# Twelve more fields looked up by one-hot rows in place of gathers, small buffers in shared homes

## The reference, cut to what matters

```python
e = stack([tbl_f[ids[:, f]] for f in range(39)], axis=1)      # 512 x 39 x 16
x0 = xk = e
for W in (W0, W1):                                            # two layers, 128 outputs each
    xk = einsum('bid,bjd,ijh->bhd', x0, xk, W.reshape(39, -1, 128))
    outs.append(xk)
z = sum(concatenate(outs, axis=1), axis=-1)                   # 512 x 256
h = concatenate([z, dense_ctx], axis=1)
h = maximum(h @ W_top1 + b_top1, 0); h = maximum(h @ W_top2 + b_top2, 0)
y = h @ W_top3
```

## Time and profile before

| what | value |
|---|---|
| median of 3 runs | 377.59 us (377.39 to 378.48) |
| span of the profiled execution | 376.0 us |
| TensorE busy | 227.8 us (61%) |
| VectorE, ScalarE busy | 159.5 us, 156.7 us (42% each) |
| GpSimd busy | 110.4 us (29%), nearly all in 115 gathers of 958 ns |
| first select of the loop on TensorE | 173.95 us |
| granted clock of TensorE | full in all 40 slices |

### The profile page before, as it was taken

One profiled execution on the slowest core, in us unless ns is written; L12 is line 12 of the kernel. 1 busy time (PEld: TensorE's weight loads), 2 busy tenths in 40 slices (PEclk: granted clock), 3 DMA queues, 4 the chain that ended last, 5 costly groups with the idle time before them and its releaser, 6 DMA issues.

```text
span 376.0 us, 4521 instructions
## 1 busy us (share of the span) xinstructions
PE 227.8 (61%) x1601; PEld 173.6 (46%) x1601; DVE 159.5 (42%) x313; ACT 156.7 (42%) x302; POOL 110.4 (29%) x119
## 2 busy tenths in 40 slices
PE   4311101001000010168999899998999999999997
PEld 4200000000000000055667588766778877788897
DVE  4350000000100000037989676897775767756411
ACT  4600000000200000027789766797786677865511
POOL 5777777777777775000000000000000000000000
PEclk9999999999999999999999999999999999999999
DMA  6800000000000000000921000000000000000000
GB/s 177 239 12 9 7 7 6 7 6 7 6 7 6 7 6 6 0 0 3 260 86 40 0 3 2 1 2 0 3 1 2 0 2 2 2 2 0 2 0 2
DMA packets 8218, 8.71 MB, mean 23 GB/s; under 512 B 2951, under 2 KB 5804, under 8 KB 8196
## 3 DMA queue, kind: packets, MB, share of 16 engines
q1 hardware_dynamic: 4516, 7.48, 7.0%
q0 software_dynamic: 3680, 0.95, 2.7%
HBM read 8.42 MB, written 0.00 MB: 22 GB/s over the span
## 4 chain that ended last, share of the span: by engine, by line
PE 50%; issue 36%; ACT 6%; DVE 4%; another core or an unknown queue 2%; DMA 1%; ACTq 0%; DVEq 0%
PE turn_bank L524 10%; PE pair_bank L445 5%; PE x_bank L469 5%; PE g_bank L502 5%; PE x_bank L471 4%; PE x_bank L472 4%; DVE onehot L771 2%; ACT prod_hi L1006 2%; PE g_bank L686 2%; PE x_bank L481 2%; PE turn_bank L562 2%; ACT prod L1001 2%; PE turn_bank L535 1%; PE x_bank L695 1%
## 5 line engine op out<-in xcount | busy, mean ns | idle before, releaser
L420 POOL DMA_INDIRECT emb<-tbl,ids_sb x115 | 110.2, 958 | 37.2 <-issue 34.7
L1001 ACT ACTIVATE prod<-pair_bank 128x512 f32<-128x512 f32 (+1 forms) x112 | 65.8, 599 | 40.8 <-PE pair_bank L445 36.0
L843 DVE TENSOR_TENSOR prod_lo<-prod,prod_hi 128x512 fp32r<-128x512 f32 x96 | 64.8, 685 | 2.7
L469 PE MATMUL x_bank<-prod_hi,pair_w_hi 128*128 128x512 f32 (+1 forms) x112 | 63.1, 564 | 1.8 <-DVE prod_lo L843 1.3
L445 PE MATMUL pair_bank<-x,sel 117*128 117x512 bf16 (+1 forms) x112 | 42.8, 384 | 0.9 <-ACT x L983 0.7
L524 PE MATMUL turn_bank<-g_sb,w_sb 128*128 128x128 f32 x312 | 42.2, 278 | 0.0
L524 PEld LDWEIGHTS turn_bank<-g_sb,w_sb 128*128 128x128 f32 x312 | 39.4, 191 | 3.1 <-issue 1.4
L686 PE MATMUL g_bank<-tab_parts,onehot 125*128 125x96 bf16 x36 | 7.4, 251 | 54.5 <-issue 54.5
L1006 ACT ACTIVATE prod_hi<-prod 128x512 fp32r<-128x512 f32 x64 | 40.1, 626 | 0.1
L471 PE MATMUL x_bank<-prod_lo,pair_w_hi 128*128 128x512 f32 x96 | 37.8, 394 | 0.0
L472 PE MATMUL x_bank<-prod_hi,pair_w_lo 128*128 128x512 f32 x96 | 37.7, 392 | 0.0
(11 more groups left out here) (140 smaller groups left out, 333.4 us busy)
## 6 DMA issues: line engine op xcount, KB each, us to landing
emb<-tbl,ids_sb POOLq DMA_INDIRECT x115
tab<-small SPq DMA_DIRECT2D x2, 560.0 KB
wt<-w_top SPq DMA_DIRECT2D x2, 512.0 KB, 4.5
tab<-small SPq DMA_DIRECT2D x1, 504.0 KB
wa<-pair_w_a SPq DMA_DIRECT2D x1, 448.0 KB
wb<-pair_w_b SPq DMA_DIRECT2D x1, 448.0 KB
wtd<-w_dense SPq DMA_DIRECT2D x1, 256.0 KB
dense_sb<-dense_t SPq DMA_DIRECT2D x1, 256.0 KB
```

The costliest lines, as they stand in the source:

```text
L420: pool.indirect_dma_start(out=emb[:, at:at + D], out_offset=None, in_=tables[f], in_offset=bass.IndirectOffsetOnAxis(ap=ids_sb[:, c * M + ...
L469: mm = pe.matmul(x1_banks[k % 2][:, :], pair_w_hi[p, t, :], hi(n), start=(t == 0), stop=(t == FULL))
L843: dve.tensor_tensor(lo(n), prod[rows, n % RING, :], prod_hi[rows, n % RING2, :], ALU.subtract).then_inc(lo_done, 1)
L1001: act.activation(prod[0:ROWS[t], n % RING, :], pair_bank[n % 2][0:ROWS[t], :], ACT.Square).then_inc(sq_done, 1)
```

## The change

Four more fields of chunk 1 (12 in all) and eight of chunk 3 (where there were none) are looked up; chunks 0 and 2 stay. `PARTS` says how many parts of four fields a chunk has. The gathers of these fields fall away. The loop of chunk 0 gets a third part, read from the second table set, whose parts now stay in memory (`tab_parts1`); the loop of chunk 2 gets two parts. The ids of 28 slots are turned, in groups of eight: two groups in the head as before, two more (eight and four slots) into `turn_bank` at steps n = 8 and n = 10, each copied by ScalarE one step later. The joins of a chunk (`words`) are one call over all its parts, in block j = number of parts at t = 3. z2, h1 and y move into `emb`, h2 into `dense_sb`, the looked-up words of later chunks into `rest`, and the summed pair weights into the early region, where buffers of the loop come later. ScalarE's copy of a looked-up part gets a wait for the split of the chunk before.

```diff
-LOOKED = (3, 1, 1, 0)
+PARTS = (0, 3, 2, 2)
+LATE_AT = (NT + 1, NT + 3)
+SLOTS = LATER * sum(PARTS)
+HEAD_SLOTS = 16
...
         def first_gathered(c):
-            return (0, 8, 16, NS)[LOOKED[c]]
+            return LATER * PARTS[c] if c else NS
...
+            def spread_later(q, bank):
+                for s in range(8 * q, min(8 * q + 8, SLOTS)):
+                    c = [s < LATER * sum(PARTS[:n + 1]) for n in range(NCH)].index(True)
+                    f = s - LATER * sum(PARTS[:c])
+                    mm = pe.transpose(halved(bank)[:, s % 8 * CH:(s % 8 + 1) * CH],
+                                      half_h[:, c, f:f + 1].to_broadcast([128, SP]), eye_h[:, :])
+                mm.then_inc(later_spread, 1)
...
-                if c + 1 < NCH and LOOKED[c + 1]:
-                    if j in (0, 1) and t == NT - 1:
+                if n in LATE_AT:
+                    pe.wait_ge(dense_act, 2)
+                    pe.wait_ge(later_ids_ok, HEAD_SLOTS // 8 + LATE_AT.index(n))
+                    spread_later(HEAD_SLOTS // 8 + LATE_AT.index(n), turn_bank)
+                if c + 1 < NCH:
+                    if j < PARTS[c + 1] and t == NT - 1:
                         wait(pe, x1_done, n // NT)
                         look_up_later(c + 1, j, 0, 2)
-                    if j in (1, 2) and t < 2:
+                    if 1 <= j <= PARTS[c + 1] and t < 2:
                         look_up_later(c + 1, j - 1, 2 * t + 2, min(2 * t + 4, HOT))
...
-                if looks and j < 2 and t >= 2:
+                if j < looks and t >= 2:
                     later_one_hot(c + 1, j, t - 2)
-                if looks and j == 2 and t == 4:
+                if looks and j == looks and t == 3:
                     words(0, c + 1)
...
+            def keep_later_ids(q, bank):
+                act.wait_ge(later_spread, q + 1)
+                s0, s1 = 8 * q, min(8 * q + 8, SLOTS)
+                act.activation(later_ids[:, s0:s1, :].rearrange("p w b -> p (w b)"), halved(bank)[:, 0:(s1 - s0) * CH],
+                               ACT.Copy).then_inc(later_ids_ok, 1)
...
+                if n - 1 in LATE_AT:
+                    keep_later_ids(HEAD_SLOTS // 8 + LATE_AT.index(n - 1), turn_bank)
...
             def keep_looked_later(c, part):
-                act.wait_ge(later_row, HOT * (2 * (c - 1) + part + 1))
+                act.wait_ge(later_row, HOT * (nth(c, part) + 1))
+                act.wait_ge(split_done, pieces(c - 1))
```

More of the change, by code:

```diff
@@ L122, in build_tower @@
         rest = sb("rest", [128, M * D])
+        later_looked = rest[:, 0:LATER * max(PARTS) * E].rearrange("b (f q d) -> b f q d", q=3, d=D)
         parts = sb("parts", [128, D, 3, M], BF16)
@@ L320, in lookups @@
         def lookups(c):
-            return sum(LOOKED[:c + 1])
+            return len(SETS) + sum(parts > 0 for parts in PARTS[:c + 1])
         def gathers(c):
@@ L465, in layer1 @@
                     c, j = divmod(k, NB)
-                    if j in (1, 2) and c + 1 < NCH and LOOKED[c + 1]:
+                    if c + 1 < NCH and 1 <= j <= PARTS[c + 1]:
                         pe.wait_ge(picked, picks(c + 1, j - 1))
@@ L665, in _ @@
                 if f == 7:
[L667 to L671, removed]
+                    for q in range(HEAD_SLOTS // 8):
+                        spread_later(q, later_id_bank[q])
             for n in range(len(SETS)):
@@ L800, in words @@
             def words(n, c=0):
[L802 to L806, removed]
+                f0, w = (0, LATER * PARTS[c]) if c else SETS[n][:2]
+                done = lookups(c) if c else n + 1
+                dve.wait_ge(picked, picks(c, PARTS[c] - 1) if c else n + 1)
+                low, words_in = (later_low[:, 0:w * D], later_looked[:, 0:w, :, :]) if c else (
+                    low_word[:, f0 * D:(f0 + w) * D], looked[:, f0:f0 + w, :, :])
                 dve.scalar_tensor_tensor(low.rearrange("b (f d) -> b f d", d=D), words_in[:, :, 2, :], 256.0,
@@ L885, in step @@
                 splits = j == 3 and c + 1 < NCH
-                looks = c + 1 < NCH and LOOKED[c + 1]
+                looks = PARTS[c + 1] if c + 1 < NCH else 0
                 seam = c in SEAMS and j == 0
@@ L1119, in keep_looked_later @@
                                looked_rows(later_bank(part), LATER, 0), ACT.Copy).then_inc(looked_ok, 1)
[L1121 to L1127 removed]
+            for q in range(HEAD_SLOTS // 8):
+                keep_later_ids(q, later_id_bank[q])
             keep_table(0)
```

52 lines of the change are left out of this document (24 added, 28 removed).

## The result

| | before | after |
|---|---|---|
| median of the runs of this comparison | 377.49 us (376.73 to 378.48, 4 runs) | 365.47 us (364.69 to 366.17, 4 runs) |
| ratio, 95% interval | | 0.968 (0.966 to 0.970) |
| profiled span | 376.0 us | 363.8 us |
| first select (the loop begins) | 173.95 us | 156.98 us |
| first select to the end of the span | 202.05 us | 206.8 us |

A forecast was written before the change was run, and what follows sets the result against it. Bound by a prologue where gathers in progress slow TensorE's look-ups, then a TensorE-bound loop and tail. 376.0 - 14.5 + (0.6 + 0.7) + 1.0 + 2.0 = 365.8 us span; with 1.6 more, 367.4 us; range 364 to 373.6.

The forecast's parts named there:

- The reading of two parts: Whole span: a prologue ending near 166 us, then a TensorE-bound loop and tail of some 205 us; the change touches both.
- Part 1: Prologue: twelve gathers fewer end TensorE's slow look-up steps sooner, a gain of 14.5 us.
- upper bound of 16.2: Prologue: gain if the work left after the last gather shrinks in proportion to the gathers, by 1.7 us.
- rival (b): Prologue: the slow stretch after the last gather shrinks with the number of gathers; gain 16.2, 365.7 us; 20%.
- Parts 2 and 3: Chunk 0's loop: chunk 1's third part of look-ups adds 0.6 and 0.7 us, twelve ids turned add 1.0 us.
- The late joins: Chunk 0's loop: joins one step ahead of ScalarE's first split, which waits for them; up to 1 us more.
- part 3: Chunk 0's loop, block j=1: twelve ids turned there, +1.0 us, between 0.7 and 2.2.
- Part 4: Chunk 2's loop: two parts of look-ups for chunk 3 on a full TensorE, +2.0 us.
- Edits without a price: Buffers moved into dead homes and ScalarE's added wait cost nothing; a real wait would delay squares, 0.6 us each.
- (a): Prologue: slow stretch not caused by the gathers, so only the loop's 4.3 us remain: 381.9 us, slower; 7%.
- (c): Chunk 0's loop turns to VectorE and ScalarE; 7.5 us in the loop for 4.3: 370.6 us; 13%.
- (d): Prologue's end: each further look-up left costs a slow step: 370.4 us; 8%.

The follow-up runs named there:

- e5: Changed kernel, no edit, on an occasion when the kernel before took 235.67 us: 234.52 us, ratio 0.998.
- e10: Changed kernel without chunk 3's look-ups, GpSimd waiting for the head's look-ups before gathers of chunks 1 to 3: 361.45 us (before 377.21).
- e12: Changed kernel with four small memsets, each waited for, behind each gather of chunks 1 to 3: 282.01 us, ratio 0.747 (before 377.10).
- e11: Changed kernel, no edit, run a third time: 365.47 us, ratio 0.969 against the kernel before.
- e7: Changed kernel without chunk 1's third part, so only chunk 3's eight fields are added: 233.39 us, ratio 0.995 (before 234.66).
- e9: Kernel before, no edit, traced on an occasion when it ran fast: 234.81 us.
- e4: Kernel before, with TensorE waiting for the last gather's landing before its first look-up: 367.54 us (before 236.18 on that occasion).

## Why the prediction was right, point by point

**The reading of two parts** stands: the head ended 17.0 us sooner, the loop and tail grew by 4.8, and the change followed from the difference. It would have been another verdict with the head short (e5: 0.998). The prediction took the long head for a property of the kernel; it is one of the occasion, and no row of the one trace could have told that.

**Part 1, 14.5 us forecast, 17.0 measured**, and just outside its upper bound of 16.2. The direction was right, and that the hold ends with the gathers, as e10 shows; that it is their being in progress that holds fell with e12. The term was small by 2.5 us in three places. (i) The end of GpSimd's work came 16.0 us sooner and not 15.0, for the twelve gathers at 1.25 us are 15.0 and one gather of 2.38 us at 23.03 us in the trace of before was 1.39 us in that of after. (ii) The stretch behind the last gather did not stay at 16.7 us but came to 15.6, as rival (b) had it (14.9 or so). (iii) Behind the look-ups the way to the first select took 6.9 us and not 7.9. Against them 31 look-ups were left when TensorE came free, not 23, 0.5 us. This last term and (iii) belong together: from the moment TensorE is free to the first select it is 9.4 us before (18 look-ups left), 9.6 after (31) and 9.2 in e11 (13), so the forecast's 0.09 us for each look-up left hardly shows. The first two have one rule behind them, which the forecast had in hand and didn't use. From the first gather to the moment TensorE is free:

| | first gather | free from | gathers | us per gather |
|---|---|---|---|---|
| before | 2.92 | 164.52 | 115 | 1.405 |
| after | 2.90 | 147.39 | 103 | 1.403 |
| e11, the same kernel | 2.90 | 147.54 | 103 | 1.404 |
| e10, up to the gate | 2.92 | 22.84 | 14 | 1.42 |
| e10, behind the gate | 28.66 | 165.68 | 97 | 1.41 |

Issued each 1.25 us and worked off each 1.40 us, a gather adds 0.15 us to a backlog, 17 to 18 us of it after 115 (16.7 us behind the end of the last one in before, 15.6 and, in e11, 15.0 after 103, 14.4 after e10's 97). By this each of twelve gathers is worth 1.405 us, 16.9 us in all, and the measured end of the slow steps moved by 17.1. (The last row's 165.68 us is the first select after a gap, not the end of single steps.) The step of TensorE, 2.80 us, is twice the 1.40, and 0.70 is half of it. In e12 the rule gives the point of freedom too: fifteen gathers up to 21.29 us are worked off at 3.02 + 15 x 1.405 = 24.1 us, three more issued at 23.14, 25.00 and 26.86 bring it to 28.3, and the next comes at 28.72, so the backlog ends at about 28.3 us; the single steps end between 27.85 and 28.58. The figures fit; that a backlog of this kind exists is inferred from them, no row shows one.

**Rule against row.** The Trainium skill's page "SBUF — State Buffer", section "Who interferes with whom", by which TensorE and ScalarE wait for no one and a DMA doesn't contend with a compute engine, would have made the head's gain 0. As far as the SBUF's ports go the trace says nothing against it; as a forecast of this kernel it fails, since e10 shows TensorE, VectorE and ScalarE all held, and e10 and e12 show them free when the gathers stop or come further apart. That something fills up and then holds the engines is the kind of thing that the Trainium skill's page "NOTIFIC — the notification-queue block", section "7.1 Overflow: three behaviours, one of which stalls the engine", describes; whether it is that block no run here shows (the missing records under what stays open bear on it).

**Parts 2 and 3, chunk 0's loop:** j=2 +0.6 forecast, +0.62; j=3 +0.7, +0.63; j=1 with the ids turned +1.0, +0.93, the block 9.33 us for "near 9.4". The late joins, kept in the range for 1 us, cost nothing. For the ids (part 3) the size was right and its sum was not, so that number is luck. The forecast had TensorE do 1.3 us more, 9.1 us of 9.4; it was busy 8.68 us of 9.33, as the transposes take 0.46 us for eight here and 0.86 us in the head. e7, with eight ids, has the same 9.33 us with TensorE busy for 8.28. What both have is ScalarE's copy of eight ids (1.02 us), and TensorE waits behind it: in e7 for the kept first layer (`x1h`), 0.99 us for 0.49 in before, and in the kernel after for the copy itself, ahead of the second group of ids:

```profile
39.31 0.65 PE L491 MATMUL x_bank<-idf,x1h 128*128 128x128 f32 x4 [0.99 <-ACT x1h L1042]
169.19 0.41 PE L532 MATMUL turn_bank<-eye_h,half_h 128*125 128x128 f16 x4 [0.53 <-ACT later_ids L1072]
```

**Part 4:** +2.0 forecast, +2.4 measured. The 12 look-up matmuls more in block j=2 (105 for 93) made 0.61 us there and the first part's start 0.69 in j=0, but j=1, into which the first part's end and the second part's start fall, grew by 1.10: I had counted one wait of 0.25 us for both parts, and the measure asks for nearer two. **Edits without a price** had none that a row shows: chunk 1, chunk 3 and the tail are as before to 0.1 us. These tenths, 0.2 us together, are what the blocks above leave of the 4.8.

**The rivals.** (a), a slow stretch not the gathers', fell with the result and again with e10 and e12. (b), the stretch shrinks with the number of gathers, was nearest in time, 365.7 for 365.5 us, and right in its mechanism for the head; the forecast of 367.4 was within the range and 1.9 us off. (c) and (d) didn't come: each block stayed within 0.1 us of its forecast in chunk 0, though in j=1 the copy of (c) was at work, and the look-ups left at the end went through freely, none at a slow step.

**What stays open.** What it is that works off 1.40 us per gather on one occasion and never shows on another: the same chip had both on different occasions. The traces point at the recording itself. A landing of a gather is 16 updates of a semaphore. Of these the trace of before holds 219 of 1840 and that of after 185 of 1648; those of the short head hold nearly all (e9 1823 of 1840, e4 all 1840), so that a median of 2.4 us from gather to landing can be read for e9 and none for before. The trace of e12, which has a stretch of either kind, holds 33 of some 272 up to 28 us and 998 of 1376 behind. Between 50 and 150 us the trace of before has 143 updates of any semaphore, one each 0.70 us, which is the grid of TensorE's steps and half of the 1.40; that of e4 has one each 0.08 us between 50 and 140 us. Every execution on record has a span and a clock, so each was recorded while it ran, and the hold and the loss of records may be one thing. That is not shown, and whether an execution that nobody records has the long head, and this change its gain, no run tells. The gathers' data are not what is worked off: the queues moved nothing from 150 us on, and of their packets before's trace has as many as e9's, while the steps went on to 164.5 us (windows of before, columns as above):

```profile
150.00:152.00 2.00, 0.09 (x1) 0.10 (x1) 0.00 (x0) 0.00 (x0) 0.00 (x0) 1.00 0.00 0
160.00:164.50 4.50, 1.24 (x5) 0.52 (x5) 0.00 (x0) 0.00 (x0) 0.00 (x0) 1.00 0.00 0
```

Open too is why the engines aren't held at once: 26 look-ups of TensorE ran freely with seven gathers issued, while VectorE stood from 7.89 to 11.60 us ahead of one-hots that it starts at 7.74 to 7.99 us in the traces of the short head, and in e10 the loop ran at half speed between 40 and 60 us before it stood. Whether e12 would lose on the short head wasn't run; as its last gather is issued at 200.8 us on either, chunk 3 would wait for it as here and the time would be near 280 us against 235, which is worked out and not measured.

## What to carry to other kernels

Where three compute engines stand still with no releaser named, count what another queue issues and divide the length of the hold by it: a constant quotient (here 1.40 to 1.42 us per gather, at 14, 97, 103 and 115 of them) points to a backlog, and here it was cured by pace as well as by number. Then ask whether the recording is part of it: count the records that such a trace should have and has not. Where before took 377 us, the changed kernel took 365.5 us, and 282.0 us with its 89 later gathers paced, a further gain of seven times the 12 us that removing twelve gathers gave; a step of 0.4 us less, still above 1.40, would bring the last gather some 35 us earlier and was not tried. And time a change on more than one occasion before you price it: the same edit was worth 3.2% and nothing.

## What the runs showed of the hardware that I had not expected

- The same kernel takes 377 or 235 us, steadily over an occasion, with no difference in the order of work. The long one shows nearly all of it as idle time between instructions, and its trace lacks most updates of semaphores (219 of 1840 for the gathers, against 1823).
- A stream of indirect gathers, one each 1.25 us, held TensorE, VectorE and ScalarE at once, for 14 to 17 us beyond the last gather; at one each 1.86 us, with memsets between them, it held none once the first backlog was gone.
- The granted clock fell to 0.5 in the idle head in one profile and stayed at 1.0 in another, with spans of 363.8 and 363.5 us.
- On the short head gathers take 0.94 us or, at times, more, up to 2.3 us (e9), and the last of 115 starts at 157.51 us and not at 146.88. In e4, where the other engines stood idle from about 18 us on, each took 0.95 us and the last started at 146.55 us.
